# Moving routing work, hid's high part and result copies in the shared expert's steps of a mixture-of-experts kernel

## The chip, the cores and the metric

The kernel runs on one core of one Trainium2 chip. The metric is the device time of one execution in microseconds (us). An execution's time is a little longer than its span, which runs from the first to the last instruction that the profiler saw. Engines are named PE (TensorE, matrix products), DVE (VectorE), ACT (ScalarE), POOL (GpSimd) and SP (SyncE); PEld is PE's loading of weights, which lies beside its products.

## The reference

The input x has 64 x 64 rows of 512 columns, so 4096 tokens of 512. Each of the 64 batches has its own 64 x 64 matrix, chosen by an index; its product with x plus a bias gives h. h goes through a mixture-of-experts layer, and the result is added to x.

```python
h = einsum('bct,bcd->bdt', x, cond_weights[itok]) + bias[itok]
scores = sigmoid(h @ gate_weight.T)              # 16 experts in 4 groups
biased = scores + expert_bias                    # best 2 groups, of them the top 4 experts
w = scores[selected] / sum(scores[selected]) * 2.5
out = sum over the 4 experts of w * (silu(h @ g.T) * (h @ u.T) @ d.T)
shared = silu(h @ shared_gate.T) * (h @ shared_up.T) @ shared_down.T
return x + out + shared
```

## The kernel before

The 4096 tokens are 32 tiles of 128. The program has three stages. In the **first** (to about 55 us) h is made, stored in DRAM, turned and scored. In the **second**, the shared expert's stage (about 55 to 209 us), the shared expert is computed for all 32 tiles; beside it DVE works out the routing, which ends in a table of token places by which POOL gathers the tokens of each expert. In the **third**, 143 tiles of gathered tokens are taken through their experts; each costs PE 4.35 us, one after another.

All engines run their own instruction list in the order written, and meet by semaphores. Products are made in split precision: a value is the sum of a high part, copied by ACT, and a low part, subtracted by DVE, so that each product is three matmuls.

**A group's steps.** The second stage has eight groups g of four tiles, and each group has four steps (`part` 0 to 3 of `shared_step(n)`, n = 4g + part), written once for each engine.

- PE: part 0 is the gate product of the hidden columns c = 0 (12 matmuls, lines L1093 to L1095), part 1 the up product of c = 0 and then the first of the four down products of the group *before* (`shared_down(g-1, 0)`, six matmuls at L1110), part 2 the other three, part 3 gate and up for c = 1. Extras follow a step: `positions` (L941), `word_tables` (L1016), and `fill_slots` (L1080) for the entries that were made one step earlier.
- ACT: `copy_shared_xT` (L727) copies high parts of x for the next group; `shared_silu(g, c)` (L799); `shared_hid_highs(g, c)` (L804) copies the high part of hid, which is silu times up; `shared_y` (L790) copies a finished result out of PSUM. There are two PSUM banks for results, so the third down product waits for the first copy. `scale_lanes` (L877) scales the entries of the table.
- DVE: `split_shared_x` (L1571) makes low parts of x; `shared_mix(g, c)` (L1579) makes hid, for which PE waits before its next up product, since that writes over the same bank; `split_shared_hid(g, c)` (L1585) makes hid's low part; `route_part(n)` runs the routing parts that `ROUTE_STEPS` names for step n; `make_entries` (L1540, L1542) makes entries by `ENTRY_STEPS`.
- SP loads the first routed expert's weights (L484) once the order of the experts is read (`read_words`, L1481), and ACT first uses them at step 18 (L708).

In ACT's step the order is:

```python
elif part == 1:
    shared_hid_highs(g, 0)
    if g > 0:
        shared_y(g - 1, 0)
...
for e in ENTRY_STEPS.get(n, ()):
    scale_lanes(e)
if part == 3:
    shared_silu(g, 1)
```

In DVE's step, for g > 0, part 1 runs the routing first and `shared_mix(g, 0)` last. Routing is done in two halves of 16 tiles; the first half's is complete before the stage but for its weights (`route_weights(0)`), which stand just ahead of step 0.

## Time and profile before

| | us |
|---|---|
| median of 3 runs | 855.01 (854.21 to 855.38) |
| the profiled execution's own time | 857.51 |
| its span | 855.7 |
| PE busy in the span | 823.3 |
| DVE, ACT, POOL busy | 487.5, 392.3, 436.2 |

The table is read as follows. The span and all rows belong to the one profiled execution. PE's busy time counts the time in which any matmul is under way; when PE waits, its next row names in brackets how long it was idle and what it waited for.

### The profile page before, as it was taken

To read this page: it belongs to the slowest core of one execution; us is meant where nothing else is said; L and a number is where in the kernel's file an instruction comes from. 1 tells how busy PE (TensorE), PEld (TensorE's weight loads), DVE (VectorE), ACT (ScalarE), POOL (GpSimd) and SP (SyncE) were. 2 spreads that over 40 slices of the span, in tenths; PEclk is the share of its full clock that TensorE was granted. 3 is DMA by queue.
4 is the path that set the end of the run, shared out by engine and by line. 5 is a ranking of instruction groups with operands and counts; after the bars stand their busy time and mean duration, and the time that the engine had idled before them with its cause. 6 is when DMAs were issued, how large, how long until landed. Compare 5 with 4: busy or idle time off the path is not lost.

```text
span 855.7 us, 19349 instructions
## 1 busy us (share of the span) xinstructions
PE 823.3 (96%) x4136; PEld 656.4 (77%) x4137; DVE 487.5 (57%) x985; ACT 392.3 (46%) x816; POOL 436.2 (51%) x400
## 2 busy tenths in 40 slices
PE   8997899999999999999999999999999999999993
PEld 5566677888788888888888888888888878878882
DVE  5688876634644445755547555647566566464440
ACT  4772366734433334533346334535455364343331
POOL 5401321155366566557655667566555675766433
PEclk9999999999999999999999999999999999999997
DMA  8971958499999999799998999799998998999754
GB/s 320 398 259 49 309 111 248 97 261 213 249 260 216 190 178 195 147 289 240 207 195 151 250 260 216 177 286 207 229 268 189 277 253 205 240 195 188 138 64 62
DMA packets 145305, 181.52 MB, mean 212 GB/s; under 512 B 30570, under 2 KB 103922, under 8 KB 142834
## 3 DMA queue, kind: packets, MB, share of 16 engines
q0 software_dynamic: 37776, 89.08, 50.7%
q1 hardware_dynamic: 106528, 80.45, 35.3%
q10 hardware_dynamic: 834, 10.49, 3.6%
q14 instruction: 150, 1.23, 0.5%
q8 instruction: 17, 0.28, 0.1%
HBM read 82.52 MB, written 67.17 MB: 175 GB/s over the span
## 4 chain that ended last, share of the span: by engine, by line
PE 80%; issue 3%; DVE 2%; DVEq 1%; ACT 1%; POOL 0%; ACTq 0%; SPq 0%
PE psGU L1052 44%; PE psY L1052 22%; PE psY L1110 4%; PE psH L931 3%; PE psGU L1093 2%; PE psGU L1095 2%; PE psGU L1094 2%; PE psM L1080 1%; DVEq L1713 1%; DVE x_ring L1542 0%; DVE entry L1540 0%; ACT y_ring L790 0%; DVE psT L1624 0%; ACT x_ring L877 0%; PE psT L1016 0%
## 5 line engine op out<-in xcount | busy, mean ns | idle before, releaser
L1052 PE MATMUL psGU<-split_w,xT_pair 128*128 x1716 | 415.9, 391 | 3.2 <-DVE xT_pair L1559 2.7
L1052 PEld LDWEIGHTS psGU<-split_w,xT_pair 128*128 128x128 f32 x1716 | 321.8, 188 | 74.5 <-issue 4.6
L650 POOL DMA_INDIRECT out<-y_ring,idx_all x143 | 231.0, 1616 | 210.6 <-SPq L539 189.5
L890 ACT ACTIVATE aT<-psGU 128x256 f32<-128x256 f32 x143 | 55.0, 384 | 337.8 <-PE psGU L1052 258.0
L1052 PE MATMUL psY<-split_w,hidT_hi 128*128 x572 | 190.5, 414 | 0.2 <-issue 0.2
L645 POOL DMA_INDIRECT tok_ring<-h_rows,idx_all x143 | 150.7, 1054 | 65.1 <-issue 42.5
L1639 DVE SCALAR_TENSOR_TENSOR aT<-aT,w_ring,psGU 128x256 f32<-128x256 f32 x143 | 67.0, 469 | 164.0 <-ACT aT L890 115.8
L1559 DVE TENSOR_TENSOR xT_pair<-psT,xT_pair 128x512 fp32r<-128x512 f32 x143 | 98.8, 691 | 65.6 <-ACT xT_pair L713 33.2
L790 ACT ACTIVATE y_ring<-psY 128x512 f32<-128x512 f32 x173 | 103.6, 602 | 20.6 <-PE psY L1110 15.9
L1052 PE MATMUL psY<-split_w,hidT_lo 128*128 x286 | 113.0, 395 | 0.0
L1052 PEld LDWEIGHTS psY<-split_w,hidT_hi 128*128 128x128 f32 x572 | 96.8, 189 | 14.0 <-issue 0.5
L1624 DVE STREAM_TRANSPOSE psT<-x_ring 128x512 f32<-128x512 f32 x143 | 102.6, 717 | 4.0 <-issue 4.0
L713 ACT ACTIVATE xT_pair<-psT 128x512 fp32r<-128x512 f32 x143 | 86.5, 605 | 6.4 <-issue 4.2
L658 POOL DMA_DIRECT2D out<-y_ring x32 | 30.1, 1135 | 114.4 <-ACT y_ring L790 110.6
L1652 DVE TENSOR_TENSOR split_w<-raw_w,split_w x42 | 51.5, 1226 | 45.1 <-ACT split_w L854 30.4
L1052 PEld LDWEIGHTS psY<-split_w,hidT_lo 128*128 128x128 f32 x286 | 53.6, 187 | 12.6
L1630 DVE TENSOR_TENSOR hidT_lo<-psH,hidT_hi 128x256 fp32r<-128x256 f32 x143 | 59.6, 417 | 0.2
L783 ACT ACTIVATE hidT_hi<-psH 128x256 fp32r<-128x256 f32 x143 | 54.2, 379 | 1.3 <-PE psH L931 1.3
L931 PE MATMUL psH<-ident,aT 128*128 128x128 f32 x286 | 54.4, 272 | 0.0
L931 PEld LDWEIGHTS psH<-ident,aT 128*128 128x128 f32 x286 | 39.5, 139 | 18.8 <-DVE aT L1639 0.4
L854 ACT ACTIVATE split_w<-raw_w x42 | 44.8, 1067 | 1.9 <-issue 1.9
L1094 PE MATMUL psGU<-split_w 128*128 128x512 f32 x96 | 37.6, 391 | 0.0
(226 smaller groups left out, 681.6 us busy)
## 6 DMA issues: line engine op xcount, KB each, us to landing
x_ring<-tok_ring SPq DMA_DIRECT2D x284, 128.0 KB
raw_w<-ffn_w SPq DMA_DIRECT2D x17, 1536.0 KB, 10.8
h_rows<-tok_ring SPq DMA_DIRECT2D x32, 256.0 KB, 9.1
out<-y_ring POOLq DMA_DIRECT2D x32, 256.0 KB
x_ring<-x_pairs SPq DMA_DIRECT2D x12, 512.0 KB, 9.2
tok_ring<-h_rows,idx_all POOLq DMA_INDIRECT x143
out<-y_ring,idx_all POOLq DMA_INDIRECT x143
h_rows<-zeros POOLq DMA_DIRECT2D x1, 2112.0 KB, 11.9
```

The costliest lines, as they stand in the source:

```text
L645: pool.indirect_dma_start(tok_ring[:, r % RING, :], None, h_rows[:, :], bass.IndirectOffsetOnAxis(idx_all[:, r:r + 1], 0)).then_inc(gather ...
L650: pool.indirect_dma_start(out[:, :], bass.IndirectOffsetOnAxis(idx_all[:, r:r + 1], 0), y_ring[:, r % YRING, :], None, compute_op=ALU.add) ...
L713: act.activation(xT_hi[:, t.slot % 2, :], psT[t.slot % 2][:], ACT.Copy).then_inc(xhi_ready, 1)
L790: act.activation(y_ring[:, s, :], psY[t.slot % 2][:], ACT.Copy).then_inc(y_ready, 1)
L890: act.activation(silu[:, t.slot % 2, :], psGU[t.slot % 2][:, 0:I], ACT.Silu).then_inc(silu_ready, 1)
L931: mm = pe.transpose(dst[:, k * P:(k + 1) * P], src[:, k * P:(k + 1) * P], ident[:])
L1052: mm = pe.matmul(dst, a[:, slot, c], w(at + col + k * H), start=(k == 0 and a is high and at == 0), stop=(k == parts - 1 and a is low))
L1094: pe.matmul(as_low, split_w[:, w:w + P], low, start=False, stop=False)
L1559: v.tensor_tensor(xT_lo[:, t.slot % 2, :], psT[t.slot % 2][:], xT_hi[:, t.slot % 2, :].bitcast(F32), ALU.subtract).then_inc(xT_ready, 1)
L1624: v.transpose(psT[t.slot % 2][:].rearrange("p (k b j) -> p k j b", k=HK, j=QUADS), x_duo[:, t.slot // DUO_TILES, :, t.slot % DUO_TILES, :] ...
L1630: v.tensor_tensor(hidT_lo[:, t.slot % 2, :], psH[:, 0:I], hidT_hi[:, t.slot % 2, :].bitcast(F32), ALU.subtract).then_inc(hidT_ready, 1)
L1639: v.scalar_tensor_tensor(out=hid[:, half, :], in0=gate, scalar=w_ring[:, w_slot, bass.ds(expert, 1)], in1=up, op0=ALU.mult, op1=ALU.mult). ...
```

## The change

In ACT's steps the copies of results now stand ahead of the high part of hid for c = 0 (which moves from part 1 to the end of part 2). In DVE's steps `shared_mix(g, 0)` stands ahead of the routing at part 1 in every group, and the low part of hid for c = 0 moves from part 2 to part 0 of the next group, behind the split of x. `route_weights(0)` moves from ahead of step 0 to step 3; the routing parts from `ties` to `tables` move one step later, `read_words` from step 15 to 16; the entries 0, 1, 2 and 4 move one step later too, and PE's `positions` and tables of words move with them. The hid of group 1, c = 0, gets another place in memory (`tok_ring` and `tok_high`), because the buffer it had is now still in use by `ties`.

```diff
--- before.py
+++ after.py
@@ -55,16 +55,16 @@
 X_CHUNK = 4
 BIG = 3.0e38
 
-ROUTE_STEPS = {0: ("groups",), 1: ("best_groups",), 2: ("top_experts",), 3: ("ties",), 4: ("counts",), 5: ("weights",),
-               6: ("ranks",), 7: ("take_turns", "starts"), 8: ("slots", "keys"), 9: ("top_slots",), 10: ("places",),
-               11: ("words",), 12: ("columns",), 13: ("tables",), 15: ("read_words",), 22: ("fill_idx",),
-               24: ("read_sp_words",)}
-ENTRY_STEPS = {10: (0,), 11: (1,), 12: (2,), 14: (3, 4), 15: (5,), 16: (6, 7), 17: (8, 9), 18: (10, 11),
+ROUTE_STEPS = {0: ("groups",), 1: ("best_groups",), 2: ("top_experts",), 3: ("first_weights",), 4: ("ties",),
+               5: ("counts",), 6: ("weights",), 7: ("ranks",), 8: ("take_turns", "starts"), 9: ("slots", "keys"),
+               10: ("top_slots",), 11: ("places",), 12: ("words",), 13: ("columns",), 14: ("tables",),
+               16: ("read_words",), 22: ("fill_idx",), 24: ("read_sp_words",)}
+ENTRY_STEPS = {11: (0,), 12: (1,), 13: (2,), 14: (3,), 15: (4, 5), 16: (6, 7), 17: (8, 9), 18: (10, 11),
                19: (12, 13), 20: (14, 15)}
 N_GROUPS = NT // ENTRIES
-PE_POS_FFN = {5: 1}
-PE_WORDS = 14
-PE_SP_WORDS = 15
+PE_POS_FFN = {6: 1}
+PE_WORDS = 15
+PE_SP_WORDS = 16
 SHARED_LOAD = 3
 SHARED_HIGH = {6: 0, 7: 1, 8: 2}
 SHARED_LOW = {11: 0, 13: 1, 15: 2}
@@ -432,11 +432,15 @@
 
         def shared_hid(g, c):
 
-            return aT[:, 1, :] if c == 1 else aT[:, 0, :] if g % 2 == 0 else ties_flat[:, 0:H]
+            if c == 1:
+                return aT[:, 1, :]
+            return aT[:, 0, :] if g % 2 == 0 else tok_ring[:, 0, 0:H] if g == 1 else ties_flat[:, 0:H]
 
         def shared_hid_low(g, c):
 
-            return aT_low[:, H:2 * H] if c == 1 else aT_low[:, 0:H] if g % 2 == 0 else ties_low[:, 0:H]
+            if c == 1:
+                return aT_low[:, H:2 * H]
+            return aT_low[:, 0:H] if g % 2 == 0 else tok_high[:, 0:H] if g == 1 else ties_low[:, 0:H]
 
         def shared_hid_high(g, c):
 
@@ -444,7 +448,7 @@
                 return hidT_lo[:].rearrange("p a i -> p (a i)")
             if g % 2 == 0:
                 return hidT_hi[:].rearrange("p a i -> p (a i)")
-            return ties_low[:, H:2 * H]
+            return tok_high[:, H + E:2 * H + E] if g == 1 else ties_low[:, H:2 * H]
 
         def is_shared(n):
             return n is not None and n < NT
@@ -796,6 +800,9 @@
                     act.wait_ge(down_done, GROUP * g)
                 elif c == 0 and g > 1:
                     act.wait_ge(down_done, GROUP * (g - 1))
+                elif c == 0 and g == 1:
+                    for k in range(2):
+                        act.wait_ge(h_stored[k], 16 * (NT // RING))
                 act.activation(shared_hid(g, c), psGU[0][:], ACT.Silu).then_inc(silu_ready, 2)
 
             def shared_hid_highs(g, c):
@@ -828,12 +835,13 @@
                 if part == 0:
                     shared_silu(g, 0)
                 elif part == 1:
-                    shared_hid_highs(g, 0)
                     if g > 0:
                         shared_y(g - 1, 0)
-                elif part == 2 and g > 0:
-                    for j in range(1, GROUP):
-                        shared_y(g - 1, j)
+                elif part == 2:
+                    if g > 0:
+                        for j in range(1, GROUP):
+                            shared_y(g - 1, j)
+                    shared_hid_highs(g, 0)
                 for e in ENTRY_STEPS.get(n, ()):
                     scale_lanes(e)
                 if part == 3:
@@ -1595,20 +1603,16 @@
                     if more:
                         split_shared_x(GROUP * (g + 1))
                     if g > 0:
+                        split_shared_hid(g - 1, 0)
                         split_shared_hid(g - 1, 1)
                 elif part == 1:
                     if more:
                         split_shared_x(GROUP * (g + 1) + 1)
-                    if g == 0:
-                        shared_mix(g, 0)
-                elif part == 2:
-                    split_shared_hid(g, 0)
-                    if more:
-                        split_shared_x(GROUP * (g + 1) + 2)
-                        split_shared_x(GROUP * (g + 1) + 3)
+                    shared_mix(g, 0)
+                elif part == 2 and more:
+                    split_shared_x(GROUP * (g + 1) + 2)
+                    split_shared_x(GROUP * (g + 1) + 3)
                 route_part(n)
-                if part == 1 and g > 0:
-                    shared_mix(g, 0)
                 if n in LOWS:
                     split_low(*LOWS[n])
                 if n == NT - 2:
@@ -1675,6 +1679,8 @@
                     elif part == "counts":
                         read_positions(NB - 2)
                         count_slots(NB - 1)
+                    elif part == "first_weights":
+                        route_weights(0)
                     elif part == "weights":
                         route_weights(NB - 1)
                     elif part == "ranks":
@@ -1713,6 +1719,7 @@
                 word = v.value_load(dve_word[0:1, bass.ds(t.done(-NT), 1)])
                 expert = word & (E - 1)
                 if n == NT:
+                    split_shared_hid(NT // GROUP - 1, 0)
                     split_shared_hid(NT // GROUP - 1, 1)
                 if n is None or n < LAST:
                     split_x(t + 1)
@@ -1735,7 +1742,6 @@
             count_slots(0)
             for n in range(GROUP):
                 split_shared_x(n)
-            route_weights(0)
             def copy_y(t):
                 s = t.slot % YRING
                 v.wait_ge(down_done, t.done(1))
```

The first place is DVE's list at the end of group 0, from the last instruction of `top_experts` on; `ties` and `mask` rows (L1192 with ties, above) are the part `ties`, w_num, w_sum and weights_te are the weights of the first half, aT<-aT,psGU is `shared_mix(0, 1)`. Before:

```order
L1303 TENSOR_REDUCE n_ties<-top_ties 128x16
L1192 TENSOR_TENSOR ties<-ties 128x16x16 x4
L1192 TENSOR_TENSOR ties<-ties,n_ties 128x16x16
L1192 TENSOR_TENSOR ties<-ties 128x16x16
L1192 TENSOR_TENSOR raw_w<-ties,above 128x256
L1579 TENSOR_TENSOR aT<-aT,psGU 128x512
L1571 TENSOR_TENSOR split_w<-kept_w,xT_pair 128x512
L1585 TENSOR_TENSOR aT_low<-aT,hidT_lo 128x512
L1346 COPY raw_w<-psM 128x256
```

After:

```order
L1311 TENSOR_REDUCE n_ties<-top_ties 128x16
L1200 TENSOR_TENSOR ties<-ties 128x16x16
L1200 TENSOR_TENSOR w_num<-raw_w,scores 128x256
L1341 TENSOR_REDUCE w_sum<-w_num 128x16
L1204 TENSOR_SCALAR w_sum<-w_sum 128x16
L1345 RECIPROCAL w_sum<-w_sum 128x16
L1200 TENSOR_TENSOR w_num<-w_num,w_sum 128x256
L1349 TENSOR_SCALAR weights_te<-w_num 128x256
L1587 TENSOR_TENSOR aT<-aT,psGU 128x512
L1579 TENSOR_TENSOR split_w<-kept_w,xT_pair 128x512
L1593 TENSOR_TENSOR aT_low<-aT,hidT_hi 128x512
L1593 TENSOR_TENSOR aT_low<-aT,hidT_lo 128x512
```

Behind it: ahead of `shared_mix(0, 1)` the part `ties` has gone and the first half's weights stand there; both low parts of hid now follow it.

The second place is ACT's list in the third group, where y_ring<-psY are result copies, x_ring<-x_ring,token_no the scaling of entries (two instructions for each entry), and aT<-aT or aT<-psGU the high part and the silu. Before:

```order
L804 ACTIVATE hidT_hi<-aT 128x512
L790 ACTIVATE y_ring<-psY 128x512
L702 DMA out<-x 16x16384
L790 ACTIVATE y_ring<-psY 128x512 x3
L877 ACTIVATE x_ring<-x_ring,token_no 128x512 x4
L799 ACTIVATE aT<-psGU 128x512
L804 ACTIVATE hidT_lo<-aT 128x512
```

After:

```order
L794 ACTIVATE y_ring<-psY 128x512
L706 DMA out<-x 16x16384
L794 ACTIVATE y_ring<-psY 128x512 x3
L811 ACTIVATE hidT_hi<-aT 128x512
L885 ACTIVATE x_ring<-x_ring,token_no 128x512 x2
L806 ACTIVATE aT<-psGU 128x512
L811 ACTIVATE hidT_lo<-aT 128x512
```

Behind it: the high part (hidT_hi<-aT) now follows the copies, and ahead of the silu of c = 1 (aT<-psGU) stand no longer the scalings of entries 0 and 1, but that of entry 0 alone, an entry that DVE now makes in the same step and no longer in the one before.

## Rows read from the trace of the kernel before

**Rows 1.** The page: busy time of each engine over the whole span

```profile
PE 823.3 (96%) x4136; PEld 656.4 (77%) x4137; DVE 487.5 (57%) x985; ACT 392.3 (46%) x816; POOL 436.2 (51%) x400
```

**Rows 2.** Windows: length; busy PE, PEld, DVE, ACT, POOL; granted clock, DMA share, GB/s

```profile
60.00:120.00 60.00, 52.36 (x226) 41.49 (x224) 48.90 (x183) 21.52 (x39) 10.93 (x11) 0.94 0.58 163
...
300.00:360.00 60.00, 60.00 (x278) 48.89 (x277) 34.36 (x61) 27.86 (x61) 34.59 (x27) 1.00 0.91 177
```

**Rows 3.** Waits, 50 to 225 us: engine, line, releaser, total, times, longest

```profile
ACT hidT_lo L804 <- DVE aT L1579: 24.5, 7, 8.0
...
PE psY L1110 <- ACT y_ring L790: 5.4, 4, 3.1
```

**Rows 4.** Timeline of TensorE, 72 to 113 us: start, duration, line, tiles, [idle before]

```profile
72.56 0.80 PE L1093 MATMUL psGU<-tok_high,split_w 128*128 128x512 f32 x1 [3.19 <-DVE aT L1579]
...
76.86 0.62 PE L1110 MATMUL psY<-split_w,hidT_hi 128*128 128x512 f32 x2
...
82.23 0.73 PE L1110 MATMUL psY<-split_w,hidT_hi 128*128 128x512 f32 x2 [1.35 <-ACT y_ring L790]
...
90.68 0.39 PE L1093 MATMUL psGU<-xT_pair,split_w 128*128 128x512 f32 x1
...
96.16 0.86 PE L1110 MATMUL psY<-split_w,ties_low 128*128 128x512 f32 x3
...
102.21 1.01 PE L1110 MATMUL psY<-split_w,ties_low 128*128 128x512 f32 x3 [3.09 <-ACT y_ring L790]
...
106.65 0.40 PE L1093 MATMUL psGU<-xT_pair,split_w 128*128 128x512 f32 x1
...
112.60 0.47 PE L1093 MATMUL psGU<-tok_high,split_w 128*128 128x512 f32 x1
```

**Rows 5.** Timeline of VectorE (DVE), 55 to 106 us, same columns

```profile
55.18 0.42 DVE L1192 TENSOR_TENSOR w_num<-raw_w,scores 128x256 f32<-128x256 f32 x1
...
57.76 0.69 DVE L1571 TENSOR_TENSOR x_low<-x_ring,tok_high 128x512 fp32r<-128x512 f32 x1 [0.42 <-ACT tok_high L727]
...
68.54 1.80 DVE L1192 TENSOR_TENSOR ties<-ties 128x256 f32<-128x256 f32 x4
...
71.81 0.69 DVE L1579 TENSOR_TENSOR aT<-aT,psGU 128x512 f32<-128x512 f32 x1
73.78 0.69 DVE L1571 TENSOR_TENSOR split_w<-kept_w,xT_pair 128x512 fp32r<-128x512 f32 x1 [1.27 <-ACT xT_pair L727]
...
77.61 0.69 DVE L1571 TENSOR_TENSOR split_w<-kept_w,xT_pair 128x512 fp32r<-128x512 f32 x1
...
81.80 0.69 DVE L1585 TENSOR_TENSOR ties_low<-ties,ties_low 128x512 fp32r<-128x512 f32 x1 [0.83 <-ACT ties_low L804]
...
85.33 0.31 DVE L1198 TENSOR_SCALAR cw_ring<-tiles_e 128x16 f32<-128x16 f32 x1
...
90.98 0.69 DVE L1579 TENSOR_TENSOR aT<-aT,psGU 128x512 f32<-128x512 f32 x1 [0.43 <-PE psGU L1095]
92.95 0.69 DVE L1571 TENSOR_TENSOR split_w<-kept_w,tok_high 128x512 fp32r<-128x512 f32 x1 [1.28 <-ACT tok_high L727]
...
101.77 0.69 DVE L1585 TENSOR_TENSOR aT_low<-aT,hidT_hi 128x512 fp32r<-128x512 f32 x1 [0.83 <-ACT hidT_hi L804]
...
104.67 0.76 DVE L1540 TENSOR_TENSOR entry<-tile_q,slot_tile 128x1152 f16<-128x1152 f16 x1
105.35 0.69 DVE L1542 TENSOR_TENSOR x_ring<-lane_q,slot_lane 128x1024 f16<-128x1024 f16 x1
```

**Rows 6.** Timeline of ScalarE (ACT), 107 to 112 us

```profile
107.35 1.32 ACT L877 ACTIVATE x_ring<-x_ring,token_no 128x512 f16<-128x512 f16 x2
...
111.01 0.58 ACT L799 ACTIVATE aT<-psGU 128x512 f32<-128x512 f32 x1
```

**Rows 7.** Timelines: SyncE's issue of routed weights, and ScalarE's first use of them

```profile
129.19 9.65 SPq L484 DMA_DIRECT2D raw_w<-ffn_w  x2
...
152.00 1.05 ACT L708 ACTIVATE split_w<-raw_w 128x1024 fp32r<-128x1024 f32 x1
```

## Prediction

> **What bounds the kernel now.** I read the page first: PE is busy 96% of the span [rows 1], so only PE's own idle or slow time can be won. The windows show where it is. From 300 to 360 us, in the routed tiles, PE has no idle time and its clock is at full speed. From 60 to 120 us, in the first groups of the shared expert, PE is busy 52.36 of 60 us and its mean granted clock is 0.94, while DVE is busy 48.90 of the 60 [rows 2]. So one stretch has slack, and in it DVE is nearly full. The waits name two kinds. ACT waited 24.5 us in all for DVE's hid before it could copy a high part, and PE waited four times, 5.4 us in all, for ACT's copy of a result [rows 3]. PE's timeline gives the places [rows 4]:
>
> - At 72.56 PE had been idle 3.19 us for DVE's `shared_mix(0, 1)`. The 12 matmuls from there to 76.86 took 4.30 us. A group product takes 2.74 us where the clock is full (90.68 to 96.16 are two, 5.48 us), 2.79 in groups with high parts in `tok_high`, so the slow clock cost 1.5 us.
> - At 82.23 it had been idle 1.35 us for a result copy. No slow stretch followed.
> - At 102.21 it had been idle 3.09 us for a result copy, and the 12 matmuls to 106.65 took 4.44 us, against 2.8: 1.65 us of slow clock.
>
> The other two waits for copies are what is left of the 5.4 us: 5.4 - 1.35 - 3.09 = 0.96 us. Altogether some 11.7 us is lost here, and more can't be won.
>
> PE's busy column alone would put the loss from 60 to 120 us at 60 - 52.36 = 7.6 us; the waits and the slow clock in that stretch come to 10.8. The Trainium skill, page "Perfetto Trace Analysis", section "Identifying the Most-Contended Engine", says that the busy share of matmuls misleads and that of the weight loads should be read: they are busy 41.49 us here and 48.89 in the steady stretch [rows 2], which would make the loss 60 x (1 - 41.49/48.89) = 9.1 us. The trace sides with the page in that the busy column is too low a ceiling.
>
> **The change, in order of time.** I walk the lists and use differences from the old times.
>
> *First wait.* DVE's list ahead of `shared_mix(0, 1)` loses the part `ties` and `split_shared_hid(0, 0)` and gains the first half's weights. `ties` begins with the second of the four instructions at 68.54 (0.46 each) and ends at 71.81: 2.8 us. A split takes 0.61 us (0.69, less the overlap with the next). The weights run from 55.18 to 0.42 before 57.76, 57.34: 2.15 us [rows 5], 2.1 with overlap. Where they stood they cost nothing and their removal wins nothing, since DVE waited for ACT at 57.76. So the mix starts at 71.81 - 2.8 - 0.6 + 2.1 = 70.5 and PE at 71.25, 1.3 earlier, after a wait of 1.9. Is this followed by a slow clock? 1.35 us was not, 3.09 was; 1.9 is nearer to 1.35, so I take none: 1.5 us more. PE ends its product at 74.05.
>
> *Down products and positions.* Both low parts of hid are now made in a row. The second ends at 73.78 - 1.3 + 3 x 0.61 + 0.1 = 74.4, so PE waits 0.35. Four down products follow (two took 102.21 - 3.09 - 96.16 = 2.96 us with a tail of nearly 0.2, so 1.39 each) without the wait at 82.23, since ACT's copies no longer stand behind the high part: to 79.95. `positions` (from 76.86 to 82.23 are two down products, the wait of 1.35, a tail and `positions`, so it takes 1.0) now stands behind them and needs `counts`. That ended at 77.61 [rows 5]; ahead of it there is 2.1 more (the weights) and 1.2 more (a split of x and `shared_mix(1, 0)` come first), so 80.9: a wait of 0.95 that is new. Then 1.0 and two products of 2.79: PE starts group 2 at 87.5 against 90.68, a gain of 3.15 (1.3 + 1.5 + 1.35 - 0.35 - 0.95 and roundings).
>
> *The entry.* To here it is a win, and the wait at 102.21 goes too: the copies that PE waits for are ahead of hid's high part, and `shared_mix(2, 0)` ahead of the routing. PE would do two products (5.48), four downs (5.56) and two products (5.46: 106.65 to 112.60 less 0.5 for one `fill_slots`) from 87.5 to 104.0. Then it needs `silu(2, 1)`. On ACT that stands in step 11 behind `scale_lanes(0)`, which needs entry 0; and this entry is now made in DVE's step 11, not 10. When does DVE get there? Before, it started the entry at 104.67. Its work up to then grows by 2.1 (weights) and shrinks by 0.6 (the low part of group 2, c = 0, is now behind it). Its waits before were 1.27, 0.83, 0.43, 1.28 and 0.83 = 4.64 [rows 5]. Now 1.27 and 1.28 remain, for copies of x behind each c = 1 mix, and before the mix at 90.98 it waits longer: `ranks` ended at 85.33, now at 85.33 + 2.1 - 0.6 - 0.83 = 86.0, while PE's product ends at 87.8. That is 1.8, in all 4.35. Entry 0 starts at 104.67 + 2.1 - 0.6 - 0.3 = 105.9 and takes 105.35 + 0.69 - 104.67 = 1.37: ready at 107.25. Scaling takes 1.3 (two instructions, 1.32) and the silu 0.6 [rows 6]: PE goes on at 109.2. **It waits 5.2 us**, the longest wait of the stage, and `shared_mix(2, 1)`, the next high part and the next splits are queued behind that same silu.
>
> That product started at 112.60. The gain there is 3.4, less 0.5 for `fill_slots(0)`, which stood ahead of it and now stands behind, less a slow clock. Two waits of over 3 us cost 1.5 and 1.65; I take 1.6 for this one. Left: 1.3 us.
>
> *Later.* The two small waits for copies (0.96) go, but the copies still stand behind the entries' scaling of the step before, as does the silu of step 19; I give back a third: +0.6. All later steps have their old work and the shorter lists; the routing's last parts (`fill_idx`, the gathers) follow PE's steps and move with them. **Sum: 1.3 + 0.6 = 1.9 us faster.** The 143 routed tiles follow at PE's pace and are moved as one. Costs of nothing: the two new waits of ACT on stored rows of h (older tiles than those for which it waited already), the other place of group 1's hid (same sizes).
>
> Against the profiled execution's own 857.5 us this gives 855.6; its median over the runs is 855.01, 2.5 lower, and the same difference from it gives **853.1 us**.
>
> **Bounds.** The clock is the least certain. After 1.9 us of idleness: 0 to 1.5 lost, of which the waits at 74 and 80 would absorb 1.3. After 5.2 us: no row is that long; 0 to 3.2 (both known slow stretches together), where below 1.6 the next entries' waits would take it up. Later waits: 0 to 0.96 given back. So the forecast's own range is a gain of 0.6 to 3.1, 851.9 to 854.4.
>
> **Rivals.**
>
> 1. *Given back.* The clock falls after the 1.9 us wait too, and longer after the long one. Net: 1.9 - 0.2 - 1.6 = 0.1 us, 854.9. For it: the two slow stretches in rows 4 began differently, one with the first matmul after the wait (72.56 took 0.80 us), the other only after some. Against: 1.35 us left no trace. The Trainium skill, page "TensorE: Matmul & The Clock Gate", Part 1, says that the chip's watch on activity runs freely and is not tied to the kernel; by that rule the slow stretches differ from run to run and this case comes up in some runs. Chance 0.20.
> 2. *The long wait is absent.* DVE reaches entry 0 in time, or the silu is not held by it. Then 5.2 + 1.6 more is won: 8.7 in all, 846.3. Against it is the order of ACT's list, which I read, and a full DVE. Chance 0.06.
> 3. *Slower: the first routed weights come late.* `word_tables` moved behind the last product of group 3, and `read_words` behind DVE's mix and three splits of step 16. The tables come later by two products (5.6) less the 1.3 won, and DVE's mix, its wait for ACT (1.28) and three splits end some 1.9 later still: 6.2 us in all, so SP issues the load at 135.4, not 129.19. Before, the second load, which waits for the first, went out 9.65 us after it, less 0.37 for the issue: 9.3 us to land [rows 7]. ACT uses the weights at 152.00, now 150.1, and the silu of step 19 is queued behind. So the margin shrinks from 13.5 to 5.4 us; from a landing time of 14.7 us on it is a wait of PE, and from 18.3 on the kernel is slower by over 0.2%. At 20 us: 5.3 late, 1.5 for the clock, less 1.9: 859.9. Against it is the 9.3 measured, with the queues as they are. Chance 0.12.
>
> **How the numbers follow.** The forecast has 0.62. A measurement of this kernel can tell about 0.2%, 1.7 us, from no change; my 1.9 stands just beyond that, so of the 0.62 I put 0.38 beyond and 0.24 within. Faster: 0.38 + 0.06 = 0.44. Within: 0.24 + 0.20 = 0.44. Slower: 0.12. The range takes the forecast's own bounds, widened by the spread of the runs and by rival 1: 850.9 to 855.9.
>
> **What would show it.** In the changed profile: PE idle about 1.9 us at 69 to 71 for the mix, about 1 us ahead of `positions`, and no wait for result copies at 80 and 99. Then one wait of about 5 us at 104 to 109 for a silu of ACT, which itself waited for x_ring<-x_ring,token_no, that is for DVE's entry. PE starts its first routed product some 1.9 us earlier. If PE goes on without a wait at 104, or ACT waits for raw_w near 150, I am wrong by rival 2 or 3.

## The result, and the profile after

The changed kernel takes 849.99 us (median of 5 runs, 847.86 to 850.68) against 855.01 us before (854.21 to 856.14): a ratio on record of 0.9935 with a 95% interval of 0.9917 to 0.9952 (the quotient of the two medians is 0.9941). It is faster by 5.0 us; 1.9 were forecast, and the time lies 0.9 us below the range. Its profiled execution took 850.37 us, with a span of 848.6.

The page's busy times and two windows, in the columns of [rows 1] and [rows 2]:

```profile
PE 822.4 (97%) x4136; PEld 656.1 (77%) x4137; DVE 486.4 (57%) x985; ACT 392.8 (46%) x816; POOL 435.5 (51%) x400
```

```profile
60.00:120.00 60.00, 53.53 (x235) 42.38 (x235) 48.54 (x181) 22.37 (x40) 11.07 (x12) 0.97 0.57 163
300.00:360.00 60.00, 60.00 (x277) 48.92 (x276) 34.68 (x60) 28.93 (x62) 34.60 (x27) 1.00 0.89 174
```

The work is the same. From 60 to 120 us PE is busy 53.53 us, not 52.36, and its weight loads 42.38, not 41.49: 1.2 and 0.9 us of 60, in line with the forecast, far from 5. The timeline of PE answers to [rows 4]:

```profile
72.28 0.50 PE L1101 MATMUL psGU<-tok_high,split_w 128*128 128x512 f32 x1 [1.78 <-DVE aT L1587]
...
81.91 0.70 PE L949 MATMUL psM<-raw_w,before 128*128 128x256 f32 x2 [0.72 <-DVE raw_w L1333]
...
109.14 0.47 PE L1101 MATMUL psGU<-tok_high,split_w 128*128 128x512 f32 x1 [3.85 <-ACT aT L806]
...
110.31 0.63 PE L1102 MATMUL psGU<-split_w 128*128 128x512 f32 x1
...
217.58 0.38 PE L939 MATMUL psH<-ident,aT 128*128 128x128 f32 x2
```

The last row is the first transposition of a routed tile; before, it stood at 219.63. So the shared stage ends 2.05 us earlier, where 1.9 was forecast. The waits are those that were named: 1.78 us for the mix (forecast 1.9), 0.72 ahead of `positions` (0.95), and 3.85 for the silu (5.2). From 110.31 on each matmul starts 0.43 us after the last, not 0.23: the slow clock behind the long wait. The chain of that wait, on DVE and ACT, answers to [rows 5] and [rows 6]:

```profile
88.97 0.69 DVE L1587 TENSOR_TENSOR aT<-aT,psGU 128x512 f32<-128x512 f32 x1 [1.71 <-PE psGU L1103]
...
105.79 0.76 DVE L1548 TENSOR_TENSOR entry<-tile_q,slot_tile 128x1152 f16<-128x1152 f16 x1
106.47 0.68 DVE L1550 TENSOR_TENSOR x_ring<-lane_q,slot_lane 128x1024 f16<-128x1024 f16 x1
```

```profile
107.19 1.33 ACT L885 ACTIVATE x_ring<-x_ring,token_no 128x512 f16<-128x512 f16 x2 [6.18 <-DVE x_ring L1550]
108.42 0.57 ACT L806 ACTIVATE aT<-psGU 128x512 f32<-128x512 f32 x1
```

Entry 0 at 105.79 (forecast 105.9), the scaling behind it after 6.18 us of waiting, the silu behind the scaling. The routed weights ([rows 7]) are issued later, at 134.89, but without a wait of ACT at their first use:

```profile
134.89 7.83 SPq L488 DMA_DIRECT2D raw_w<-ffn_w  x2
```

```profile
150.28 1.05 ACT L712 ACTIVATE split_w<-raw_w 128x1024 fp32r<-128x1024 f32 x1
```

The other 5 us between the two spans (855.7 - 848.6 = 7.1, less 2.05) are made behind the shared stage, where the forecast had nothing. The tail shows one piece. ACT's last copies and POOL's last scatters, first before the change, then after it:

```profile
838.42 0.38 ACT L783 ACTIVATE hidT_hi<-psH 128x256 fp32r<-128x256 f32 x1 [0.86 <-PE psH L931]
...
843.42 1.08 ACT L790 ACTIVATE y_ring<-psY 128x512 f32<-128x512 f32 x2 [4.62 <-issue]
```

```profile
844.33 1.56 POOL L650 DMA_INDIRECT out<-y_ring,idx_all  x1 [3.04 <-SPq L539]
846.18 1.56 POOL L650 DMA_INDIRECT out<-y_ring,idx_all  x1 [0.30 <-issue]
```

```profile
833.54 0.39 ACT L787 ACTIVATE hidT_hi<-psH 128x256 fp32r<-128x256 f32 x1 [0.85 <-PE psH L939]
835.85 0.60 ACT L794 ACTIVATE y_ring<-psY 128x512 f32<-128x512 f32 x1 [1.93 <-PE psY L1060]
836.76 0.60 ACT L794 ACTIVATE y_ring<-psY 128x512 f32<-128x512 f32 x1 [0.31 <-PE psY L1060]
```

```profile
836.76 1.56 POOL L654 DMA_INDIRECT out<-y_ring,idx_all  x1 [0.34 <-SPq L543]
838.62 1.56 POOL L654 DMA_INDIRECT out<-y_ring,idx_all  x1 [0.30 <-issue]
```

Before, ACT stands idle for 4.62 us ahead of its last two copies of results, released by nothing that the profile shows ("issue"); they start at 843.42, though PE's last product had started at 841.20. After, each follows its own product on PE: the first copy starts 0.9 us, the last 0.4 us behind the start of the last matmul of its product. From the last transposition on PE (837.97 before, 833.09 after) to the end of the span it is 17.8 and 15.5 us. The rest, 2.8 us, lies between the first and the last routed tile: in this profile of before, two tiles (112 and 122, counted from the first) took 1.4 and 1.8 us more than the usual 4.35.

In the tail itself the change edits nothing. But the two added waits on `h_stored`, the semaphores that tell that rows of h are in DRAM, make ACT's program one instruction longer (680 semaphore instructions in the trace of ACT, 679 before). That is the theory tested first.

### The profile page after: what moved, and what is told of

It reads as the page before. It is cut to its first block, busy times and chain, and to the rows that moved or that the text cites. A ratio compares the mean times of both kernels' runs of the same rounds, so it can differ in the third digit from the quotient of the medians.

```text
span 848.6 us, 19350 instructions
## 1 busy us (share of the span) xinstructions
PE 822.4 (97%) x4136; PEld 656.1 (77%) x4137; DVE 486.4 (57%) x985; ACT 392.8 (46%) x816; POOL 435.5 (51%) x400
## 3 DMA queue, kind: packets, MB, share of 16 engines
q14 instruction: 150, 1.23, 0.5%
## 4 chain that ended last, share of the span: by engine, by line
PE 84%; DVE 1%; issue 1%; ACT 0%; POOL 0%; ACTq 0%; DVEq 0%; SPq 0%
PE psGU L1060 46%; PE psY L1060 23%; PE psH L939 4%; PE psY L1118 3%; PE psGU L1101 2%; PE psGU L1102 2%; PE psGU L1103 2%; PE psM L1088 1%; POOL out L654 0%; PE psT L1024 0%; DVE entry L1548 0%; ACT x_ring L885 0%; DVE aT_low L1593 0%; DVE x_ring L1550 0%; ACT y_ring L794 0%
## 5 line engine op out<-in xcount | busy, mean ns | idle before, releaser
L939 PEld LDWEIGHTS psH<-ident,aT 128*128 128x128 f32 x286 | 39.5, 139 | 18.7 <-DVE aT L1643 0.4
```

The lines of the kernel that those rows point to most:

```text
L939: mm = pe.transpose(dst[:, k * P:(k + 1) * P], src[:, k * P:(k + 1) * P], ident[:])
```

## The experiments

**Theory L:** where ACT's code lies decides when it is fetched, and the added instruction moved it. **Theory N:** the stalls are chance. **Theory S:** all of the gain is made in the shared stage, and the profile of before was an unlucky one. Below, "stage" is the time at which the first routed transposition starts, "tail" the time from the last one to the end of the span; both are read from one profile of each kernel, while the times are medians of several runs. The kernel before ran beside each group: 855.27 us beside `e1_waits` to `e4_mix`, 855.98 beside `e5_sixteen` to `e8_tail`, 854.52 beside `e9_pair` to `e12_mixback` and 855.21 beside the last three. Each ratio is against the kernel before of its own group. The differences from the changed kernel that are given below are taken between medians of different groups, and differences between two groups of less than about 1.5 us are not clear of noise: `e7_less`, which does the same work as the changed kernel, is 6.35 us faster than the kernel before beside it, the changed kernel 5.0.

### The added instruction alone, and single edits

`e1_waits`, the kernel before with

```diff
+                elif c == 0 and g == 1:
+                    for k in range(2):
+                        act.wait_ge(h_stored[k], 16 * (NT // RING))
```

> The kernel before with nothing but the two waits on stored rows of h that the change adds to ACT's silu of group 1. They are met long before they are reached, so they are one or two instructions more in ACT's program and no time in the shared stage. The profiled runs put 2.05 us of the gain ahead of the first routed tile (219.63 to 217.58 us), 2.8 us between it and the last (before, two tiles cost 1.39 and 1.84 us more than their pace of 4.35; after, one cost 0.3) and 2.26 us behind the last product (17.77 to 15.51). Theory L (where the code lies): the routed stage and the tail lost time because instructions came late there, and the shift of ACT's program by these waits cured it. Then this kernel starts its first routed tile at 219.6 as before, but routed stage and tail are 2 to 5 us shorter: 850 to 853 us. Theory N (the stalls come and go with the moment at which the stage runs, or from one execution to the next): no effect, 855 us within 1, stalls of the old size in stage or tail. Theory S (all of the gain is made in the shared stage and only the profiled run of before was unlucky by some us): 855 too, but its profile may show a shorter tail.

852.15 us (ratio 0.9967, 0.9956 to 0.9978), stage 219.51, tail 15.7. ACT's last rows:

```profile
835.76 0.38 ACT L783 ACTIVATE hidT_hi<-psH 128x256 fp32r<-128x256 f32 x1 [0.86 <-PE psH L934]
837.88 0.60 ACT L790 ACTIVATE y_ring<-psY 128x512 f32<-128x512 f32 x1 [1.74 <-PE psY L1055]
838.97 0.60 ACT L790 ACTIVATE y_ring<-psY 128x512 f32<-128x512 f32 x1 [0.49 <-PE psY L1055]
```

Two waits that hold nothing up win 3.1 us, 2.1 of them in the tail of the profiles, and nothing moved in the shared stage. Where the other 1.0 us is made, the profiles don't show. Theory S falls, since the gain comes without any change in the stage, and N can't explain a median that is 3.1 us lower; that the place of the code is what counts is left to the runs below.

`e2_fw`, the changed kernel with

```diff
-ROUTE_STEPS = {..., 3: ("first_weights",), 4: ("ties",),
+ROUTE_STEPS = {..., 4: ("ties",),
...
+            route_weights(0)
             def copy_y(t):
```

> The changed kernel with one part undone: the first half's routing weights stand ahead of the first step again, where DVE waits for ACT anyway. By the prediction's steps they add 2.1 us to DVE's list up to entry 0 and cost nothing where they stood. So the mix of group 0 comes 1.8 to 2.1 us earlier (PE no longer waits at 72), entry 0 starts some 2 us earlier, and PE's long wait of 4.24 us at 105 to 109 shrinks to about 2. The first routed tile starts at 215.5, not 217.6. If the stage's gain passes whole to the end: 848.0 us. Theory L and theory N differ: ACT's program here is that of the changed kernel, so by L routed stage and tail keep the changed kernel's lengths (615.5 and 15.5 us); by N they may take on any length between the two (up to 618.3 and 17.8), since all runs 2 us earlier. If the weights' place is not what holds entry 0, the first tile starts at 217.6 and the time is 850.

847.78 us (0.9920, 0.9906 to 0.9933), tail 15.7, PE without a wait at 69 to 72. By the medians the first weights cost the change 2.2 us; the stage, counted from its own first product, is 159.0 us long, against 161.1 to 162.7 in four profiles of the changed order. But the long wait did not shrink to 2 us, as I had expected. It kept its size, since with the first wait gone PE comes as much earlier as the entry does:

```profile
104.66 0.77 PE L1101 MATMUL psGU<-tok_high,split_w 128*128 128x512 f32 x1 [3.88 <-ACT aT L806]
```

`e3_silu`, the changed kernel with

```diff
+                if part == 3:
+                    shared_silu(g, 1)
                 for e in ENTRY_STEPS.get(n, ()):
                     scale_lanes(e)
-                if part == 3:
-                    shared_silu(g, 1)
```

> The changed kernel with ACT's silu of the group's second product ahead of the scaling of lanes in the same step, so that it no longer waits for DVE's entry 0. The prediction named that queueing as the cause of the long wait (4.24 us in the changed kernel). Then the wait at 105 to 109 for this silu goes, PE does the mix's down product next without the slow clock of some 1.5 us, and then waits for entry 0 itself at fill_slots, which comes no earlier than before: I expect two thirds of it back there, a net 0.9 us: first routed tile at 216.7, time 849.1. If DVE's entry is late through DVE's own list, the whole 4.2 us comes back as a wait for the entry and the time is 850. If the silu alone held the stage, 4 to 5 us are won: 845 to 846. By theory L routed stage and tail stay as in the changed kernel unless the order of ACT's instructions moves its code; by N they may differ.

848.52 us (0.9929, 0.9913 to 0.9944), tail 15.8: 1.5 us better than the changed kernel by the medians, though the intervals of the two overlap for the most part (the stage, from its own start, is 160.3 us long). The wait for the silu is gone, and PE waits 0.51 and 3.05 us for ACT's scaled lanes of the next entries instead. The queueing was real, but DVE's entries are late in themselves.

`e4_mix`, the kernel before with

```diff
-                    if g == 0:
-                        shared_mix(g, 0)
+                    shared_mix(g, 0)
...
-                if part == 1 and g > 0:
-                    shared_mix(g, 0)
```

> The kernel before with one part of the change alone: DVE's shared_mix of a group's first product stands ahead of the routing part in that step for every group, not only for the first. Nothing else moves: routing keeps its old steps, the first weights their old place, ACT's list its order. By a walk through the queues PE's waits at 82 and 102 shrink since mixes, high parts and result copies all come earlier by the routing part that stood ahead of them (1.5 to 3 us each in groups 1 to 3), and entry 0 is not pushed back: a gain of 3 to 5 us in the shared stage, first routed tile at 215 to 217 against 219.6, and 850 to 852 us with the routed stage and tail as before. The rival: the parts pay only together, because the result copies still stand behind hid's high part on ACT; then under 1 us, 854 to 855. ACT's program is unchanged, so by theory L the stalls of 1.4 and 1.8 us in the routed stage and the long tail (17.8 us) stay; by N they may vanish with the earlier start.

852.88 us (0.9971, 0.9957 to 0.9985; single runs from 849.53 to 858.16). The part pays alone, 2.4 us against 3 to 5 expected. Its profile (858.16 us, the slowest of its 12 runs) has the long tail (17.9, ACT's program being unshifted) and four half-speed stretches, one of them without a wait ahead of it. Windows on PE:

```profile
115.00:125.00 10.00, 10.00 (x57) 1.00 0.37 107
125.00:132.00 7.00, 7.00 (x33) 0.76 1.10 236
```

PE is busy for all 17 us, and still the mean clock falls to 0.76 in the second window.

### Where the code lies

`e5_sixteen` and `e6_128`, the kernel before with, for 16 and for 128 copies (from step 24, 2 a step; from step 16, 8 a step):

```diff
+                if n >= 24:
+                    for k in range(2):
+                        act.activation(pads[:, (n * 2 + k) % 16:(n * 2 + k) % 16 + 1], ones[:, 0:1], ACT.Copy)
```

> The kernel before with 16 tiny copies (one element per lane, nobody reads them) on ACT, two at the end of each of the steps 24 to 31 of the shared stage, where ACT is idle for over half of the time. Measured before: routed part 618.3 us and tail 17.7 us in the kernel before; 615.5 to 616.7 and 15.5 to 15.8 in the three kernels with one instruction more in ACT's program. Theory L (the place of ACT's code decides when it is fetched): the shared stage stays at 164.2 us; routed part and tail change, and since 16 instructions are much more than one, they may become shorter or longer than in the kernel before, anything from 2 us better to 5 us worse. Theory N (it was the two waits themselves, by what they wait for): nothing changes, 855.3 us with a tail of 17.7.

> The same with 128 such copies, eight at the end of each of the steps 16 to 31. The profile shows the packets of the instruction queue as 8 KB each, which are 128 instructions of 64 bytes. Theory L, sharpened: what counts is where in such a block of 128 the code lies, so a shift by exactly one block brings back the kernel before: routed part 618 us with the same two stalls near tiles 112 and 122, tail 17.7 us, 855 us (the copies themselves cost at most 1 us in the shared stage, seen there). If the shift counts but not modulo the block, tail and routed part take other lengths. By a theory in which more code is simply slower, it is over 856.

16 copies: 851.52 us (0.9945, 0.9925 to 0.9965), stage 218.72, tail 15.9. More code, and faster by 4.5 us, of which 1.9 is in the tail; the rest isn't placed. 128 copies: 857.87 us (1.0024, 1.0011 to 1.0036), stage 222.47 (the stage is 3 us longer, not the 1 us that I had expected: from 140 us on PE waits 1.45, 0.51 and 0.47 us for result copies, where the kernel before waited 0.70 once, and the rest isn't placed), tail 17.3, with ACT's late copies back. A shift by 128 instructions restores the long tail, as theory L says. The stall at tile 122 and the 1.4 us at tile 112 did not come back with it (tile 112 took 0.7 us more than usual); that half of the expectation failed. With 16 copies the stall has moved instead of going: ACT now stands idle one copy earlier. This copy starts 0.45 us behind PE's last transposition in the kernel before, and 1.67 us behind it here.

```profile
836.76 0.38 ACT L784 ACTIVATE hidT_hi<-psH 128x256 fp32r<-128x256 f32 x1 [2.08 <-issue]
```

`e7_less`, the changed kernel with

```diff
-                if c == 1 and g > 0:
+                if c == 1 and g > 1:
                     act.wait_ge(down_done, GROUP * g)
```

> The changed kernel with one wait left out that is covered by an earlier one (ACT's silu of group 1, second product, waits for down products for which the copies of results ahead of it have waited already). The order of all work stays; ACT's program is one instruction shorter behind group 1, so its routed loop lies where it lies in the kernel before. Theory L: the stage keeps the changed kernel's gain (first routed tile 2 us earlier than before), but the tail goes back from 15.5 to 17.7 us and the routed part from 615.5 to some 618: 853 us, which is what was forecast. Theory N: 850 as in the changed kernel.

849.63 us (0.9929, 0.9911 to 0.9947), tail 15.3: as the changed kernel. The expectation, 853 us with the long tail, failed. The trace shows why: ACT still has 680 semaphore instructions. I take it that two waits fit one instruction, so nothing was taken away. It says nothing on L, but gives one more profile of the changed order.

`e9_pair`, the changed kernel with

```diff
                 elif c == 0 and g == 1:
-                    for k in range(2):
-                        act.wait_ge(h_stored[k], 16 * (NT // RING))
+                    act.wait_ge(h_stored[1], 16 * (NT // RING))
...
                 if part == 0 and g > 0:
+                    if g == 1:
+                        act.wait_ge(h_stored[0], 16 * (NT // RING))
                     shared_hid_highs(g - 1, 1)
```

> The changed kernel with one of the two new waits of ACT (on stored rows of h, slot 0) moved from the silu of group 1 to the hid copy three instructions ahead, where it is just as long met. In the last try at this (a covered wait left out) the count of ACT's instructions in the trace didn't change, so it could show nothing: two waits fit one instruction, the third makes another. Here no instruction has more than two, and ACT's program should be one instruction shorter from group 1 on, as long as in the kernel before. Theory L: the stage is the changed kernel's (161.1 us from its first product to the first routed tile, or 162.6 with a slow stretch of the clock at its start), but ACT's last two copies come late again and the tail is 17.7 us, not 15.5: 852 us, at least 2 more than the changed kernel. Theory N: tail 15.5 and 849.8.

851.96 us (0.9970, 0.9957 to 0.9982), 679 semaphore instructions, stage 217.49, tail 18.7:

```profile
834.85 0.38 ACT L787 ACTIVATE hidT_hi<-psH 128x256 fp32r<-128x256 f32 x1 [0.85 <-PE psH L940]
...
840.96 1.08 ACT L794 ACTIVATE y_ring<-psY 128x512 f32<-128x512 f32 x2 [5.72 <-issue]
```

The same order of all work, every wait met as before, one instruction less: 2.0 us slower than the changed kernel by the medians, with intervals that don't touch, and the long tail is back (its profile, 854.87 us, is the slowest of its ten runs). With `e1_waits` this shows from both sides that the count of ACT's instructions sets the tail. The two parts also add up: the order without the added instruction gains 2.6 us here, the instruction without the order gained 3.1, and 5.7 lies between the 5.0 of the changed kernel and the 6.35 of `e7_less`.

`e8_tail`, the kernel before with

```diff
+            act.activation(warm[:], ones[:, 0:1], ACT.Silu)
             copy_hidT(tile_at(LAST), LAST)
             act.wait_ge(y_ready, LAST - 1)
```

> The kernel before with one tiny activation (0.2 us, nobody reads it) on ACT behind the routed loop's last turn and ahead of the last copies, where ACT is idle for 0.9 us. Theory L: the loop's code stays where it was, so the routed part keeps its 618.3 us with the stalls near tiles 112 and 122; only the code behind is shifted by one, and ACT's last two copies come 2 us earlier, as with the two waits: tail 15.6, 853.2 us. If the tail's 2.1 us is made by the loop's place and not by the tail's own, the tail stays at 17.7 and the time at 855.3.

852.63 us (0.9966, 0.9952 to 0.9980), tail 15.7. One instruction behind the loop does all that one instruction ahead of it did (0.9967): the gain is the tail's own, and the loop's place is not needed.

What ACT probably waits for can be seen in the DMA queues (packets, MB, share of the 16 DMA engines). First two stretches of the tail before, 839.8 to 841.8 and 841.8 to 843.42, which is ACT's late copy:

```profile
q0 software_dynamic: 127, 0.25, 94.4%
q14 instruction: 1, 0.01, 2.5%
```

```profile
q0 software_dynamic: 122, 0.22, 100.1%
q14 instruction: 1, 0.01, 1.2%
```

Then two of after, 834.0 to 834.9 and 834.9 to 835.85, which is ACT's first copy:

```profile
q14 instruction: 1, 0.01, 3.7%
```

```profile
q0 software_dynamic: 29, 0.06, 76.8%
q14 instruction: 1, 0.01, 5.9%
```

q14, kind "instruction", brings code in packets of 8 KB (150 with 1.23 MB on the page). From ACT's last copy of hid (838.42) to 839.8 there is none before. In the five profiles with the long tail (before twice, `e4_mix`, `e6_128`, `e9_pair`) packets begin 1.5, then 3.3 to 4.6 and then 5.5 to 6.8 us after the last copy of hid. In after twice, `e1_waits`, `e7_less` and `e8_tail` they begin 0.6, 1.5 and 3.4 to 4.1 us after it. The records don't name the engine. One at 1.5 is in all of them, and the last of the three comes after ACT has gone on, so I take the one at 0.6 or at 3.3 to 4.6 for ACT's. The timing bears this out: in all five long tails ACT's next copy starts 0.7 to 1.2 us after that packet ends, also in `e9_pair`, where both are about 1 us later than in the rest, and in `e5_sixteen` a packet ends 1.2 us ahead of the copy that is late there.

Before, the late packet runs beside the 122 packets of POOL's scatters, on DMA engines that they keep busy all the time; in the early case it has the engines to itself. The packet itself isn't slow, it took 0.32 us there and 0.54 in the early case: what is late is its start. In `e9_pair` the scatters keep the engines 96.7% busy in the 3.1 us ahead of the stretch with the late packet and 57.2% in it. Why one instruction makes 3 us, the DMA's load or a copy that ACT must first finish, wasn't separated. That ACT waits for code at all is argued from the order of these events; what the runs show is that the count of instructions ahead of the last copies decides.

The Trainium skill, page "Advanced Engine Details and Errata", section "ISA Cache", gives lines of 16 KB for 256 instructions, and only two of them. An estimate from that page's figures is 64 bytes for an instruction, so that 128 of them are one 8 KB packet; `e6_128`, which restored the tail, agrees with that. Whether one packet is a whole line or half of one, no run here shows.

### Kernel or execution

`e14_before` and `e15_after` are the two kernels, profiled again.

> The kernel before itself, profiled a second time on this chip, to tell what belongs to a kernel from what belongs to one execution. By theory L the late last copies of ACT belong to the kernel: tail 17.5 to 18.7 us again. The two stalls of 1.39 and 1.84 us in the routed part (near tiles 112 and 122) may or may not: the kernels with the shifted code had stalls of 0.3 to 1.6 us in some of the same tiles. If they come back at the same tiles with the same size they are the kernel's; if the routed part is 616 to 617 us they were that execution's.

> The changed kernel itself, profiled a second time. Tail 15.3 to 15.8 us by theory L. The routed part was 615.5 us in the first profile, the shortest of all; if it is 616 to 617 here, the 2.8 us between the two first profiles in this part were mostly chance. The half-speed stretch at 55 to 58 us should be absent if the clock's stretches differ from run to run: stage 161.1 instead of 162.6 us.

PE's waits with the largest total (total, times, longest) between first and last routed tile, 225 to 826 us, of before, then of before's second profile, then of after's second:

```profile
PE psGU L1052 <- DVE xT_pair L1559: 2.7, 2, 1.6
```

```profile
PE psGU L1052 <- issue: 0.3, 1, 0.3
```

```profile
PE psGU L1060 <- DVE xT_pair L1567: 1.6, 1, 1.6
```

The routed part took 618.3 us in the first profile of before and 616.2 in the second; 615.5 and 617.8 in those of after. The stalls change with the execution: 1.4 us at tile 112 and 1.8 at 122, then 0.4 at 31 and 0.6 at 112; 0.3 at 112, then 0.3 there and 1.9 at 96. Tile 112 is slow in every profile of every kernel here, by 0.2 to 1.6 us, so its place is fixed and its size is chance; what makes it wasn't looked for. None of it separates the two kernels. The tails are the kernels' own: 17.8 and 17.6 us before, 15.5 and 15.5 after. The half-speed stretch at 55 us is gone in the second profile of after. One at 71 us, behind the first wait, stands in its place, but the 0.72 us wait ahead of `positions` goes with it, and the stage ends at 216.08, not 217.58. The second profile of before has a longer slow stretch at 100 us instead (windows, 60 to 120 us):

```profile
60.00:120.00 60.00, 52.52 (x220) 41.35 (x218) 48.11 (x181) 21.50 (x38) 10.93 (x11) 0.91 0.58 163
```

```profile
60.00:120.00 60.00, 54.35 (x235) 43.43 (x233) 50.03 (x185) 22.48 (x40) 11.72 (x12) 0.94 0.55 151
```

### Undoing and going on

`e12_mixback`, the changed kernel with `shared_mix(g, 0)` behind `route_part(n)` again for g > 0:

> The changed kernel with one part undone: DVE's shared_mix of a group's first product stands behind the routing part again in groups 1 and on. The kernel before with this part alone was 2.4 us faster than before. If the part also pays among the others: slower than the changed kernel by about as much, 852. By a walk through the queues it doesn't: in the changed kernel counts and entry 0 are what PE waits for, and a routing part that stands ahead of the mix comes earlier by that mix and its wait; the wait ahead of positions goes from 0.7 to 0.3, the copies of results that wait in group 2 come in time, and the stage is 1.3 us shorter: 848.7.

```diff
-                    shared_mix(g, 0)
+                    if g == 0:
+                        shared_mix(g, 0)
...
                 route_part(n)
+                if part == 1 and g > 0:
+                    shared_mix(g, 0)
```

848.73 us (0.9925, 0.9910 to 0.9940), 1.3 us faster than the changed kernel by the medians, 0.9 by the ratios, with intervals that overlap. So a part that won 2.4 us alone wins nothing among the others; whether it costs something there isn't shown. With the copies ahead of hid's high part PE no longer waits for them, which is what the early mix was for.

`e10_both`, the edits of `e2_fw` and `e3_silu` together:

> The changed kernel with both of the single edits that were measured before: the first weights ahead of step 0 (847.8 us) and the silu ahead of the scaling of lanes (848.5). If the waits that they take away are different ones, their gains over the changed kernel add: 2.1 + 0.9 to 1.5, so 846.5 to 847 us. If they are one chain (both make entry 0 less pressing), the second brings nothing: 847.8. The wait of PE at 69 to 72 should be gone and in place of the 4.2 us at 105 there should be waits for entries at fill_slots of 1 to 3 us. Tail 15.5 to 15.8 by theory L, since ACT's program is as long as in the changed kernel.

```diff
-ROUTE_STEPS = {..., 3: ("first_weights",), 4: ("ties",),
+ROUTE_STEPS = {..., 4: ("ties",),
...
+                if part == 3:
+                    shared_silu(g, 1)
                 for e in ENTRY_STEPS.get(n, ()):
                     scale_lanes(e)
```

845.72 us (0.9895, 0.9876 to 0.9913), the fastest of all, 8.8 us or 1.05% under the kernel before and 4.3 under the changed one, about the sum of the two (3.7), with an interval clear of the changed kernel's. What PE still waits for are the lanes of entries 0 and 1:

```profile
104.71 0.70 PE L1088 MATMUL psM<-entry,x_ring 128*128 128x144 f16 x8 [0.51 <-ACT x_ring L885]
...
112.69 1.14 PE L1088 MATMUL psM<-entry,x_ring 128*128 128x144 f16 x8 [3.06 <-ACT x_ring L885]
```

`e11_old_steps`, the changed kernel with `ROUTE_STEPS`, `ENTRY_STEPS` and PE's steps of before, `route_weights(0)` ahead of step 0, and the silu ahead of the lanes:

> The changed order of products of hid and of copies, but with all of routing, the entries and PE's word tables in the steps that they have in the kernel before, the first weights ahead of step 0, and the silu ahead of the scaling of lanes. Entry 0 is then made a step earlier, as before, so PE's wait of 4.2 us for the silu behind it goes without another of its size: I expect 4 to 5 us less in the stage than in the changed kernel, some waits of 1 to 2 us left, 845 to 846 us. The other view: moving routing a step later was needed, since DVE is full from 60 to 110; then positions or the group products of step 5 to 9 wait for DVE instead, and the time is 848 to 850.

```diff
-ENTRY_STEPS = {11: (0,), 12: (1,), 13: (2,), 14: (3,), 15: (4, 5), ...
+ENTRY_STEPS = {10: (0,), 11: (1,), 12: (2,), 14: (3, 4), 15: (5,), ...
...
-PE_POS_FFN = {6: 1}
+PE_POS_FFN = {5: 1}
```

846.52 us (0.9902, 0.9884 to 0.9920), 3.5 us faster than the changed kernel, with the stage ending at 211.65, the earliest of all, and a routed part of 618.0 us in its profile, among the longest, which by the scatter above is chance. It is as fast as `e10_both` within noise, so with this order routing did not have to move.

`e13_three`, `e10_both` with the edit of `e12_mixback`:

> The changed kernel with all three edits that were faster than it one by one: first weights ahead of step 0, the silu ahead of the scaling of lanes, shared_mix of a group's first product behind the routing part in groups 1 and on. The first two together gave 845.7 us. If the third takes away its own waits here too (0.7 us ahead of positions, 0.2 to 0.4 us for copies of results in groups 2 and 3), some 0.8 us more: 845 us, first routed tile 157 us behind the stage's first product, tail 15.2 to 15.8. If the waits for entries at 104 and 110 take all of that, 845.7 as without it.

846.23 us (0.9898, 0.9870 to 0.9925; 843.70 to 850.31), no better than without the third edit: PE's wait of 0.72 us ahead of `positions` is gone, but the waits for entries are as long (0.58 and 3.07 us).

## Why the prediction was right and wrong

- **First wait: right.** 1.9 us forecast, 1.78 measured, in all four profiles of the changed order (after twice, `e7_less`, `e9_pair`). That the clock stays up behind it is partly luck: it does in three of these four, but it falls in the profiles of `e3_silu` and `e12_mixback` (0.88 from 66 to 80 us), which have the same wait.
- **Positions and the missing wait for copies: right.** 0.72 us against 0.95, no wait for a copy at 82. In `e7_less` PE starts group 2 at 86.49, which is 87.51 on the time of [rows 5] against 87.5 forecast. The bracket behind the gain of 3.15 adds up to 2.85, not 3.15; the times themselves give 3.2.
- **Entry 0 and the long wait: right in mechanism, wrong in size.** The wait is 3.85 us against 5.2 (3.87 in the second profile), 1.3 too long, because the entry was put 1.2 us too late. That entry 0 read 105.79 against my 105.9 is luck: this execution had a slow stretch at 55 us which made all of it some 1.5 us late. In `e7_less`, without it, entry 0 starts at 103.63; its stage began 1.02 us earlier than before's (54.39 against 55.41), so 104.65 on the time of [rows 5]. Summing DVE's list by groups for both kernels shows where my "grows by 2.1 and shrinks by 0.6" missed a term: before, four tiny instructions from 87.5 to 88.6 and two at 89.4 took together 1.0 us more than in `e7_less`. One of them, beside POOL's issue, and the same one in `e7_less`:

```profile
87.72 0.83 DVE L1398 CAST e_int<-e_rows 128x16 int32<-128x16 f32 x1
```

```profile
86.83 3.16 POOL L665 DMA_DIRECT2D h_rows<-weights_te  x1
```

```profile
92.86 0.17 DVE L1406 CAST e_int<-e_rows 128x16 int32<-128x16 f32 x1
```

  This cast of 128x16 takes 0.83 us while POOL issues `h_rows<-weights_te`, and 0.17 without it. Not every issue does this: before, another cast of 128x16 at 84.80 took 0.17 while POOL issued other transfers. In the changed order that issue falls ahead of DVE's wait of 1.7 us for PE, which absorbs it (there another cast of 128x16 takes 0.94 us beside it). That the issue is what slows DVE was read from the two traces, not tried.
- **The clock: right in the difference, with luck.** I took 3.15 us lost before and 1.6 after, 1.55 less. The windows from 50 to 120 us give a mean clock of 0.95, 0.93, 0.93 and 0.93 for the four profiles of the old order, and 0.95, 0.95, 0.98 and 0.95 for the new: 9.1 against 6.0 us at half speed, so 4.6 against 3.0 us lost, 1.6 less. Both amounts are 1.4 us over mine, and single profiles of one order differ as much as the two orders do (0.95 and 0.95 in the two first profiles), so that the difference came out to 0.1 us is luck. The Trainium skill, page "TensorE: Matmul & The Clock Gate", Part 1, says that the watch on activity isn't tied to the kernel. The slow stretch that came at 55 us in one execution of the changed kernel and not in another agrees, and so does that of `e4_mix`.
- **The stage in all.** The four profiles of the old order (before twice, `e1_waits`, `e8_tail`) end it at 219.33 us on average (218.70 to 219.63), the four of the new (after twice, `e7_less`, `e9_pair`) at 216.65 (215.45 to 217.58): 2.7 us earlier, 0.1 of it a different start, against 1.9 forecast. The term of the sum that was mis-sized is the entry's (1.2 us). But this excess of 0.8 us alone would have left the time in the range.
- **The step that failed: "The 143 routed tiles follow at PE's pace and are moved as one."** The tiles do, within the stalls of an execution (616.97 us on average in the four old-order profiles, 616.52 in the four new). What follows the last of them doesn't: the tail is 2.2 us shorter. With 2.7 this makes 4.9 of the 5.0 us. `e1_waits` has the tail's gain without the new order (3.1 us, 2.1 of them in the tail), `e9_pair` the new order without the tail's gain (2.6 us). The prediction put the two waits of ACT under "Costs of nothing", since they are met; it asked what they wait for, not what they are: an instruction. Without that one instruction the forecast would have held: `e9_pair`, which has both waits but no added instruction, took 851.96 us, inside its range. Why the instruction is worth this much stays open beyond what the packets suggest.
- **Rivals.** Given back: the clock fell behind the first wait too in one profile of four (three of six with `e3_silu` and `e12_mixback`), and the gain was there all the same, since the wait ahead of `positions` takes up part of such a stretch, as the prediction's bounds had it. The long wait absent: no. The first routed weights late: the issue came at 134.89 (135.4 forecast), and nobody waited.

## What to carry to other kernels

Look at long idle times with the releaser "issue" near the end of an engine's program and at the instruction queue beside them: any edit that adds or drops one instruction ahead of the place can win or lose as much there as a reordering does. So before a gain is put down to an edit, run the edit with its instruction count held, and the count without the edit. Parts of a reordering needn't add: undo each one in the final order, since one that won alone may win nothing there.

## What was not expected of the hardware

- One more instruction in ACT's program, at either of two places ahead of its last copies, took 2.1 us off the tail; 16 more took 1.9 off (15.9 us), and 128 more did not (17.3 us). Instruction packets on q14 are of 8 KB, and where the late one runs before the change, data keeps the DMA engines 94 to 100% busy.
- PE's half-speed stretch can come with no wait ahead: 0.76 mean clock from 125 to 132 us in `e4_mix`, behind 10 us in which PE was busy all the time at the full clock. The 12 runs of this kernel spread over 8.6 us.
- A tiny DVE instruction took 0.83 us beside one of POOL's issues of a DMA, 0.17 without it; beside others of POOL's issues one of the same size took 0.17.
